# Fused transformer block: attention keys projected once, probabilities in a ring of four, a batch's projections allowed into the next iteration

## The reference, cut to what matters

```
x = x + 0.5 * _L0_ffn_ref(_layernorm(x, axis=-1), ...)
x = x + _L0_attn_ref(_layernorm(x, axis=-1), ...)
x = x + 0.5 * _L0_ffn_ref(_layernorm(x, axis=-1), ...)

def _L0_ffn_ref(x, theta, phi, theta_noise, phi_noise):
    real = jnp.einsum('bti,io->bto', x, jnp.cos(theta + theta_noise))
    imag = jnp.einsum('bti,io->bto', x, jnp.sin(phi + phi_noise))
    return jnp.sqrt(real * real + imag * imag)

def _L0_attn_ref(q, Wq, Wk, Wv, Wo):
    xq = rope(q @ Wq)
    xk = rope(kv @ Wk)
    xv = kv @ Wv
    xk = jnp.repeat(xk, 2, axis=-1)
    xv = jnp.repeat(xv, 2, axis=-1)
    ...
    scores = jax.nn.softmax(xq @ xk * scale, axis=-1)
    out = (scores @ xv).transpose(0, 2, 1, 3).reshape(batch, seq_len, -1)
    return out @ Wo
```

## Time and profile before

| | before |
|---|---|
| median of three runs | 2628.72 us |
| profiled execution: time | 2626.98 us |
| profiled execution: span | 2625.2 us |
| TensorE busy, share of the span | 84% |
| VectorE | 71% |
| ScalarE | 56% |
| GpSimd | 55% |
| mean granted TensorE clock | 0.948 |

### The profile page before, as it was taken

The page is one execution under the profiler, slowest core; times in us unless marked ns, Lnnn a source line. Parts: engine busy times, 40 slices in busy tenths (PEclk is TensorE's granted clock), DMA queues, the critical chain, the costliest instruction groups (busy, mean ns, idle before and its releaser), DMA issues. The chain is left out here.

```text
span 2625.2 us, 39867 instructions
## 1 busy us (share of the span) xinstructions
PE 2217.7 (84%) x13956; PEld 1037.1 (40%) x13956; DVE 1855.0 (71%) x4540; ACT 1458.5 (56%) x2779; POOL 1453.0 (55%) x1312
## 2 busy tenths in 40 slices
PE   2689988988988998998898984689999999998487
PEld 1223323323323332332332322356656666665343
DVE  5777776776777777777677732378778877787487
ACT  2166566566566656656656662465565565654164
POOL 2365665665666566566556540355565655555266
PEclk9799999999999999999999996799999999999699
DMA  3221112112111111211211101000000000000121
GB/s 112 53 47 45 37 37 53 32 32 51 37 37 41 45 37 33 57 25 39 51 37 26 44 5 44 6 13 9 13 13 9 17 9 13 13 5 5 35 58 45
DMA packets 73286, 86.91 MB, mean 33 GB/s; under 512 B 9216, under 2 KB 59520, under 8 KB 72960
## 3 DMA queue, kind: packets, MB, share of 16 engines
q1 hardware_dynamic: 73088, 84.37, 12.8%
HBM read 21.16 MB, written 12.58 MB: 13 GB/s over the span
## 5 line engine op out<-in xcount | busy, mean ns | idle before, releaser
L320 DVE TENSOR_REDUCE mS<-ps 128x1 f32<-128x512 f32 x1024 | 676.9, 681 | 301.8 <-PE ps L655 297.5
L452 ACT ACTIVATE pr<-ps 128x512 f32<-128x512 f32 x1024 | 585.7, 597 | 388.0 <-PE ps L639 368.1
L518 POOL TENSOR_TENSOR prs<-pr 128x512 f32<-128x512 f32 x384 | 488.0, 1291 | 247.5 <-ACT pr L452 247.5
L639 PE MATMUL ps<-qst,kst 97*128 97x512 f16 x1024 | 396.8, 391 | 54.0 <-ACT pr L452 52.8
L655 PE MATMUL ps<-kst,qst 96*128 96x512 f16 x1024 | 400.0, 392 | 37.2 <-DVE mS L320 26.4
L677 PE MATMUL ps<-pr,vt 128*32 128x512 f32 x2048 | 278.7, 617 | 0.0
L639 PEld LDWEIGHTS ps<-qst,kst 97*128 97x128 f16 x1024 | 99.0, 98 | 418.1 <-ACT pr L452 308.1
L522 POOL TENSOR_TENSOR terms<-terms 128x512 f32<-128x512 f32 x128 | 162.9, 1272 | 88.7 <-DVE terms L313 88.7
L313 DVE TENSOR_TENSOR terms<-ps,rope 128x512 f32<-128x512 f32 x256 | 173.2, 678 | 35.0 <-POOL lo L527 29.9
L527 POOL TENSOR_TENSOR lo<-terms,hi 128x512 f16<-128x512 f32 x128 | 148.4, 1159 | 76.9 <-ACT hi L432 76.9
L655 PEld LDWEIGHTS ps<-kst,qst 96*128 96x128 f16 x1024 | 101.0, 99 | 151.3 <-DVE mS L320 81.3
(11 more groups left out here) (264 smaller groups left out, 4558.2 us busy)
## 6 DMA issues: line engine op xcount, KB each, us to landing
qst<-hi SPq DMA_DIRECT2D x128, 128.0 KB, 2.4
kst<-hi SPq DMA_DIRECT2D x128, 128.0 KB, 2.4
qst<-lo SPq DMA_DIRECT2D x64, 128.0 KB, 2.4
kst<-lo SPq DMA_DIRECT2D x64, 128.0 KB, 2.4
x<-in_q SPq DMA_DIRECT2D x16, 256.0 KB, 2.8
rope<-in_rope SPq DMA_DIRECT2D x1, 4096.0 KB, 12.6
x<-yold SPq DMA_DIRECT2D x16, 256.0 KB, 2.5
m_x<-x SPq DMA_DIRECT2D x16, 256.0 KB, 2.8
```

Source lines behind the costliest of these rows:

```text
L320: v.tensor_reduce(mS[:, b % 2, t, s:s + 1], ps[:, 2 + n % 2, :], AX, ALU.max).then_inc(S["s_read"], 1)
L452: a.activation(pr[:, s % 2, g, :], ps[:, g % 2, :], ACT.Exp, scale=ATT_SCALE).then_inc(S["exp"], 1)
L518: g.tensor_tensor(prs[:, c, :], pr[:, 0, c, :], pr[:, 1, c, :], ALU.add).then_inc(S["prs"], 1)
L639: mm(ps[:, g % 2, :], kst[:, h, P * kt:P * kt + P], qst[:, h, :], start=True, stop=True).then_inc(S["st"], 1)
```

## The change

Keys: `Wk` is laid out so that the even and the odd members of the pairs lie in groups of their own, and each of four key groups is projected once. VectorE still makes 16 products a batch: each key group is read twice, with the cosine and with the sine, and `rotated` adds or subtracts. `hi` and `lo` of the keys then hold even and odd members apart, and `stack` puts them in place with 12 transfers of 16 rows for four heads where it had 3 of 32 rows. The columns of `Wq` are permuted to match.

Probabilities: `pr` has four places and `prs` two; all eight pairs are added by GpSimd, and `denominators_directly` is gone. Rounds of `values` stand in slots 4s + 7 for even and 4s + 5 for odd s. `yold` becomes the second half of `x8`, which pays for the room.

Order: the table has new numbers, slots may run past 63 into the next iteration (`staged`, `due`), the maxima lag by 10 slots, and the waits for banks 4 and 5 are now made by `take`, which waits for the last reader of the bank. The core of the diff:

```diff
 ATTENTION_AT = {
 
-    "values": (0, 1, 7, 8), "output": 4, "x2": 4, "stats1": 5, "aggr1": 8, "xn1": 11, "turn1": 16, "evac1": 17,
-    "ffn": 18, "squares": 19, "ffn_b": 22, "squares_b": 22, "sqrt": 25, "resid": 25, "stats2": 27, "aggr2": 29,
-    "xn2": 31, "turn2": 36, "evac2": 35, "gate": 37, "gate_in": 37, "gate_top": 41, "gate_count": 45,
-    "project": (37, 38, 39, 40, 41, 42, 45, 46, 47, 49, 50, 51, 53, 56, 59, 60), "high_lag": 3, "low_lag": 2,
-    "denominators_lag": 3, "maxima": 5,
+    "values": (4, 6, 11, 15), "output": 13, "x2": 13, "stats1": 14, "aggr1": 15, "xn1": 20, "turn1": 26, "evac1": 26,
+    "ffn": 28, "squares": 27, "ffn_b": 28, "squares_b": 28, "sqrt": 28, "resid": 28, "stats2": 30, "aggr2": 31,
+    "xn2": 36, "turn2": 41, "evac2": 41, "gate": 42, "gate_in": 42, "gate_top": 46, "gate_count": 51,
+    "project": (43, 44, 45, 47, 48, 49, 51, 52, 53, 54, 56, 58),
+    "product": (44, 45, 46, 47, 48, 49, 51, 52, 53, 54, 56, 57, 58, 61, 64, 67), "high_lag": 2, "low_lag": 1,
+    "pv": (7, 5), "numerators": 17, "dev1": 18, "dev2": 33, "add_squares": 27, "add_squares_b": 28, "xnl": 43,
+    "denominators": 13, "divide": 25, "maxima": 10,
 }
...
-        pr = sb("pr", [P, 2, NT, SEQ])
+        pr = sb("pr", [P, 4, NT, SEQ])
...
-        prs = sb("prs", [P, NG, SEQ])
+        prs = sb("prs", [P, 2, NG, SEQ])
...
-        product_at = {q + 1: m for m, q in enumerate(AT["project"])}
-        rotated_at, high_at, low_at = ({q + lag: m // 2 for m, q in enumerate(AT["project"]) if m % 2}
-                                       for lag in (1, AT["high_lag"], AT["low_lag"]))
-        assert max(high_at) < SLOTS
+        def staged(slots):
+
+            at = {}
+            for n, q in enumerate(slots):
+                at.setdefault(q % SLOTS, []).append((q // SLOTS, n))
+            return at
+
+        values_at = staged(AT["pv"][s % 2] + NT * s for s in range(HEADS))
+        numerators_at, division_at = (staged(AT[n] + NG * NT * j for j in range(NG)) for n in ("numerators", "divide"))
+        denominators_at = staged(AT["denominators"] + 2 * NT * n for n in range(HEADS // 2))
+
+        project_at, product_at = staged(AT["project"]), staged(AT["product"])
+        rotated_at, high_at, low_at = (staged(q + lag for q in AT["product"][1::2])
+                                       for lag in (0, AT["high_lag"], AT["low_lag"]))
+
+        def due(at, i, q, stage=2):
+
+            return [(i - late - stage, n) for late, n in at.get(q, ()) if 0 <= i - late - stage < BATCH]
...
-            return 16 * 6 * ((NG * b + j) // HEAD_GROUPS + 1)
+            return 16 * 15 * ((NG * b + j) // HEAD_GROUPS + 1)
...
                 def stack(b, j, kq):
                     r = slice(DH * j, DH * j + DH)
                     g0 = NG * ring(b, j)
-                    dst, rows = ((qst, (hi, lo, hi)), (kst, (hi, hi, lo)))[kq]
-                    for row, src in enumerate(rows):
-                        sp.dma_start(dst[DH * row:DH * row + DH, g0:g0 + NG, :],
-                                     src[r, kq]).then_inc(S["stacked", ring(b, j)], 16)
+                    if kq == 0:
+                        for row, src in enumerate((hi, lo, hi)):
+                            sp.dma_start(qst[DH * row:DH * row + DH, g0:g0 + NG, :],
+                                         src[r, 0]).then_inc(S["stacked", ring(b, j)], 16)
+                        return
+
+                    for row, src in enumerate((hi, hi, lo)):
+                        for odd in range(2):
+                            for s in range(2):
+                                d, r0 = DH * row + DH // 2 * odd, DH * j + DH // 2 * s
+                                sp.dma_start(kst[d:d + DH // 2, g0 + s:g0 + NG:2, :],
+                                             src[r0:r0 + DH // 2, 1, odd:NG:2]).then_inc(S["stacked", ring(b, j)], 16)
...
                 def product(b, m):
                     p, c = m // 2, m % 2
-                    kq, g = p // NG, p % NG
-                    dve.wait_ge(S["pair"], 4 * NG * b + m + 1)
+                    if p < NG:
+                        n, table = m, NG * c + p
+                    else:
+
+                        a, odd = (p - NG) // 2, p % 2
+                        n, table = 2 * (NG + a) + c, 2 * NG + 2 * (odd ^ c) + a
+                    dve.wait_ge(S["pair"], 3 * NG * b + n + 1)
                     if c == 0 and 2 * NG * b + p >= 2:
                         dve.wait_ge(S["lo"], 2 * NG * b + p - 1)
-                    v.tensor_tensor(terms[:, p % 2, c, :], ps[:, 4 + c, :], w["rope"][:, 2 * kq + c, g, :],
+                    v.tensor_tensor(terms[:, p % 2, c, :], ps[:, 4 + c, :], w["rope"][:, table, :],
                                     ALU.mult).then_inc(S["pair_free"], 1)
...
                 def exponentials(b, s, g):
                     head = HEADS * b + s
-                    if g == 0 and head >= 2:
-                        act.wait_ge(S["pv"], head - 1)
-                    if 2 <= s < HEADS - 2 and s % 2 == 0:
-                        act.wait_ge(S["prs"], NG * ((HEADS // 2 - 2) * b + s // 2 - 1) + g + 1)
-                    if s >= HEADS - 2 and g == 0:
-                        act.wait_ge(S["dd"], NT * b + s + 3 - HEADS)
-                    if s < 2 and b and g == 0:
-                        act.wait_ge(S["dd"], NT * b - 1 + s)
+                    if g == 0 and head >= 4:
+                        act.wait_ge(S["pv"], head - 3)
+                    if head >= 4 and s % 2 == 0:
+                        act.wait_ge(S["prs"], NG * (head // 2 - 2) + g + 1)
                     n = SLOTS * b + NG * s + g
                     act.wait_ge(S["st"], n + 1)
-                    a.activation(pr[:, s % 2, g, :], ps[:, g % 2, :], ACT.Exp,
+                    a.activation(pr[:, s % 4, g, :], ps[:, g % 2, :], ACT.Exp,
...
                 def add_pair(b, n, c):
-                    pairs = (HEADS // 2 - 2) * b + n
+                    pairs = HEADS // 2 * b + n
                     pool.wait_ge(S["exp"], SLOTS * b + NG * (2 * n + 1) + c + 1)
-                    if pairs:
-                        pool.wait_ge(S["dn"], pairs)
-                    g.tensor_tensor(prs[:, c, :], pr[:, 0, c, :], pr[:, 1, c, :], ALU.add).then_inc(S["prs"], 1)
+                    if pairs >= 2:
+                        pool.wait_ge(S["dn"], pairs - 1)
+                    k = 2 * (n % 2)
+                    g.tensor_tensor(prs[:, n % 2, c, :], pr[:, k, c, :], pr[:, k + 1, c, :], ALU.add).then_inc(S["prs"], 1)
 
                 def rotated(b, p):
                     pool.wait_ge(S["pair_free"], 2 * (2 * NG * b + p + 1))
                     g.tensor_tensor(terms[:, p % 2, 0, :], terms[:, p % 2, 0, :], terms[:, p % 2, 1, :],
-                                    ALU.add).then_inc(S["rot"], 1)
+                                    ALU.subtract if p >= NG and p % 2 == 0 else ALU.add).then_inc(S["rot"], 1)
...
-                def project(i, p, c):
-                    kq, g = p // NG, p % NG
-                    if c == 0 and p == 0:
+                def project(i, n):
+
+                    p, c = n // 2, n % 2
+                    if n == 0:
                         pe.wait_ge(S["xnl"], i + 1)
-                        if is_old(i):
-                            pe.wait_ge(S["gate_read"], i - 2)
-                    if p:
-                        pe.wait_ge(S["pair_free"], 4 * NG * i + 2 * p - 1 + c)
-                    wt = [w["wq"][:, h, g, c, :] if kq == 0 else w["wk"][:, h, c, P * g:P * g + P] for h in range(2)]
+                    take(4 + c, "pair_free", 4 * NG * i + (n + 1 if p < NG else 2 * n - 5 - c))
+                    wt = [w["wq"][:, h, p, c, :] if p < NG else w["wk"][:, h, P * (n - 2 * NG):P * (n - 2 * NG) + P]
+                          for h in range(2)]
...
                 def denominators(b, n):
-                    pe.wait_ge(S["prs"], NG * ((HEADS // 2 - 2) * b + n + 1))
+                    pe.wait_ge(S["prs"], NG * (HEADS // 2 * b + n + 1))
                     if n % 2 == 0 and NG * b + n:
                         pe.wait_ge(S["den"], NG * b + n // 2)
                     for g in range(NG):
-                        ins = mm(ps[DH * g:DH * g + DH, 7, :], w["ones"][:, 0:DH], prs[:, g, :],
+                        ins = mm(ps[DH * g:DH * g + DH, 7, :], w["ones"][:, :], prs[:, n % 2, g, :],
                                  start=n % 2 == 0, stop=n % 2 == 1, skip_group_check=True)
                     ins.then_inc(S["dn"], 1)
-
-                def denominators_directly(b, s):
-                    kt = s % NT
-                    if kt == 0:
-                        pe.wait_ge(S["den"], NG * b + NG - 1)
-                    for g in range(NG):
-                        ins = mm(ps[DH * g:DH * g + DH, 7, :], w["ones"][:, 0:DH], pr[:, s % 2, g, :],
-                                 start=kt == 0, stop=kt == NT - 1, skip_group_check=True)
-                    ins.then_inc(S["dd"], 1)
...
```

(25 more changed lines are left out.)

114 lines of the change are left out of this document (57 added, 57 removed).

## The result

The changed kernel takes 2711.48 us (median of four executions, 2708.75 to 2715.3); the kernel before, on the same chip, 2629.12 us (2628.07 to 2629.76). The ratio is 1.0315, 95% interval 1.0297 to 1.0333: 3.15% slower. The profiled execution took 2715.3 us, 88.3 more than the profiled one of before.

What follows compares the result with a forecast made beforehand. TensorE's work binds before, then a loop through slot 10's scores: steps sum to 92.9 us, plus 2 for half clock, 94.9 per iteration. 2627 + 12 + 4 = 2643 in the profile, 2645 as median; range 2592 to 2690.

Steps and rivals of the forecast that it cites:

- the ramps: Iterations before and behind the 13: first scores 5 us later, next iteration 1, savings and tail counted, sum +4 us.
- the loop through slot 10: Slot 10's scores await the last key transfer, holding up output projection and next keys: 94.9 us per iteration; chance 0.42.
- 1, landing to output projection, and half clock: TensorE's scores, guard transposes, value projection, a round, attention matmuls: 3.9 us, plus 2 us for 1.2 GHz.
- 1, output projection: TensorE's output projection after the attention matmuls: 3.85 us.
- 2, to the transposes: Residual, maxima, statistics, aggregation, deviations, normalisation with exponentials, first transposes: about 13.4 us.
- Step 3: Feed-forward lap in slot 28, square root, second statistics, normalisation and transposes, up to the first projection: 24.9 us.
- Step 5: Twelve key transfers on SyncE's queue, 11 pitches of 0.55 us plus 2.4 us landing: 8.4 us, ends 7.6 and 9.2.
- the forecast wait of 5.6 us: TensorE comes to slot 10's scores 5.6 us before the keys land, 41.2 us after the first projection.
- the three waits for `hi`: GpSimd before the last `lo`: three waits of about 0.8 us where a `lo` directly follows its rotation, 2.4 in all.
- GpSimd and the clock cost more: Late `hi` copies on ScalarE delay exponentials and additions, both waits bring low clock: 98 us per iteration, 2685; chance 0.14.
- step 4: First projection to last `lo`, bound by GpSimd's rotations, `lo`, additions and waits: 38.4 us.
- The loop is shorter: Issues at 0.47 us, `hi` waits closed, clock high: 90.5 us per iteration, 2587, deciding below 93.3; chance 0.33.

Runs made afterwards that it cites:

- `maxima` 14: Changed kernel with the scores for the maxima lagging 14 slots instead of 10: 2614.65 us, second time 2613.7 us, ratio 0.9937.
- the short sums: GpSimd's last two pair sums of a batch cut to 32 of 512 columns: 2693.29 us in the changed kernel, 2599.53 us with the maxima's scores lagging 14 slots.
- the kernel with 2606.78 us: Changed kernel with the maxima's scores lagging 14 slots instead of 10 and the even members' key transfers issued first: 2606.78 us, ratio 0.9913.
- `pv` 6, 5: The kernel with 2606.78 us with the values' rounds at `pv` (6, 5) in place of (7, 5): 2632.27 us, ratio 1.0006.

## Why the prediction was wrong

The direction was right, the size was not: 2711.48 us lies over the range's 2690. Per iteration 4.1 us are missing, 54 us over the 13, and in the ramps 19: together the 72 us between the 2643 that were forecast for the profile and its 2715.3. The forecast's mechanism, the loop through slot 10, was the right one, and the runs with `maxima` 14 and with three transfers show it. It gave +0.9 us per iteration and +4 for the ramps; measured were +5.0 and +22.6. Step by step, in us, means over eleven iterations of the changed kernel:

| step of the loop | predicted | measured |
|---|---|---|
| 1, landing to output projection, and half clock | 0.1 + 3.9 + 2 | 0.05 + 6.28 |
| 1, output projection | 3.8 | 3.84 |
| 2, to the transposes | 13.4 | 13.93 |
| 3, to the first projection | 24.9 | 27.20 |
| 4, to the last `lo` | 38.4 | 38.78 |
| 5, the transfers | 8.4 | 9.06 |
| sum | 94.9 | 99.1 |

**Step 3 failed most, by 2.3 us.** Its terms as they stand there add up to 25.5, not 24.9: 0.6 is an error of addition. Copies to square root (1.2 + 3.8 + 0.7 + 1.28 + 1.06) were 8.04 as summed. Residual to deviations took 5.8 for 5.5. The stretch of deviations, normalisation and transposes, 2.5 + 4.6 + 1.1 = 8.2 in the sum, took 10.2: the copy of numerators, up to 1.67 us late behind a values' round at half clock, pushes the normalisation. The prediction expected TensorE to wait about 4 us after the root (3.0 was measured), and priced it at nothing in the loop. The run without the root took 1.2 of these 2.0 us away, and the iterations of the changed kernel that keep full clock there take 8.98 us, so half clock is those 1.2 us and the other 0.8 are a sum that was too short. The last stretch, transposes to projection, was 0.65 shorter than summed.

**Step 5 was mis-sized.** The pitch, from the start of one issue to the next, is 0.64 us for 32 KB; I took 0.55, and even my bound of 0.62 was too low. The trace of before had the value, in the rows behind those of the earlier trace rows:

```profile
972.86 0.60 SPq L209 DMA_DIRECT2D qst<-hi  x1
973.50 0.60 SPq L209 DMA_DIRECT2D qst<-lo  x1
974.14 0.60 SPq L209 DMA_DIRECT2D qst<-hi  x1
```

These 128 KB transfers start 0.64 us apart. The two rows that I read (971.03 to 972.22) hold the first of the burst, which took 0.55, so they give 0.60 a transfer and not 0.62; and 0.47, my lower bound, is what some of the loads at the program's start take, not the first key transfer of a burst. In the changed kernel the queries' 128 KB transfers start at 1043.14 and 1043.77, 0.63 apart: from 32 to 128 KB the size made no difference to the pitch. The landing is 2.0 us after the issue, not 2.4. The Trainium skill (DMA: Bandwidth & Descriptors, Rules for kernel authors) says that under 64 KB one pays mostly overhead and should coalesce; this case agrees: cutting a transfer in four leaves the pitch of each as it was. The 9.2 us that the prediction gave for that rule is the measured 9.06 within 0.2.

**Steps 1, 2 and 4 held**, each within 0.6 us, and so did the forecast wait of 5.6 us (6.08), the half clock after it and the three waits for `hi`. TensorE got 28 matmuls an iteration less, and nothing of that reached the time, since it then waited for the loop.

**The ramps failed by 19 us.** I put 4 where 22.6 were. The scores of the first three batches start at 79.6, 159.9 and 251.3 us, before at 75.3, 140.7 and 227.8: 4.3 us later, then another 14.9, then another 4.3. The second lap is the large one, for which I had 1 us. Twelve transfers in the kernel before make these starts 6.1, 10.0 and 12.1 us later, so the transfers alone are about half; with three transfers in the changed kernel the second lap, from 73.8 to 148.5, still takes 74.7 us against 65.4, so the new order of slots costs some 9 there, of which 4.7 are left at the third start. What in the order does that was not tried.

**The rivals.** "GpSimd and the clock cost more" (98 us, 2685) was nearest in the time, and half of it is true: low clock after both waits. Its GpSimd half is not, as step 4 came out at 38.8 and the short sums give only 1.2 us. "The loop is shorter" needed 93.3 us. My chance of 0.14 for the case over 97 us was too small, since I summed each step from durations with few waits among them, and but for the 0.1 between landing and scores every step came out at or over its sum.

## What to carry to other kernels

When a change lets work run into the next iteration, look for the first instruction on the in-order engine that waits for its end: if the work that starts the next lap stands behind that instruction, everything between is one loop, and saved work elsewhere gives nothing. The cure can be one slot number. A loop summed from busy times came out too short here in almost every step: look for what stands ahead of each step in its engine's own order, and for waits with half clock behind them. Cutting a transfer into n costs n - 1 issues of the queue (0.64 us each here). A steady iteration may have slack for them (4.9 of 5.7 us here); the ramps had less, and the third batch started 12.1 us late.

## What the runs showed of the hardware

- The pitch of issues on SyncE's queue was the same for both sizes: 0.64 us for 32 KB, 0.63 to 0.64 for 128 KB. The landing differed a little, 2.0 and 2.4 us after the issue.
- Waits of 2.00 and 1.88 us were followed by 3.3 to 3.4 us at a granted clock of 0.50; with a wait of 3.00 us in the kernel with 2606.78 us went 6.8 us of it. Less idle time in all (9.4 us for 10.3) went with more half clock (10.5 for 6.6).
- The length of a wait did not decide: the same wait of 2.99 to 3.00 us behind the root had half clock in nine of the changed kernel's 13 iterations and full clock in four, and one of 1.31 us had it in nine of 13 with `pv` 6, 5 and in none without.
- A table load on ScalarE took 1.28 us, and the root started 0.02 us after it (975.24 + 1.28, 976.54).
